# Three slots in place of two for the gathered rows of the second convolution

## What is computed

```
q = (x @ qw + qb); k = (x @ kw + kb); v = (x @ vw + vb)      # 8 heads of 16
alpha = sum(q[dst] * k[src]) / 4                             # per head
a = exp(alpha - max over dst);  a = a / (sum of a over dst)
out = segment_sum(v[src] * a, dst) + x @ sw + sb
x = layernorm(x + out)
```

## Time and profile before

| | |
|---|---|
| timed runs | 3534.03, 3537.03, 3537.83 us; median 3537.03 |
| profiled execution | span 3610.8 us, 73.8 us above the median; the page gives no other time for it |
| busy, share of the span | PE 75%, DVE 73%, ACT 56%, POOL 52% |
| the second convolution | from about 1271 to 1935 us |

### The profile page before, as it was taken

The page is one execution under the profiler, slowest core; times in us unless marked ns, Lnnn a source line. Parts: engine busy times, 40 slices in busy tenths (PEclk is TensorE's granted clock), DMA queues, the critical chain, the costliest instruction groups (busy, mean ns, idle before and its releaser), DMA issues. The chain is left out here.

```text
span 3610.8 us, 49441 instructions
## 1 busy us (share of the span) xinstructions
PE 2722.1 (75%) x14325; PEld 1795.7 (50%) x14325; DVE 2619.5 (73%) x3171; ACT 2007.5 (56%) x3400; POOL 1867.7 (52%) x1771
## 2 busy tenths in 40 slices
PE   7799999969999867777774789999999774233332
PEld 3466655646666645555553245566566553122211
DVE  6589888979999958888885159989989994222222
ACT  0166666645555547777784257788788783111111
POOL 4478776333333266666663655444553003667675
PEclk9999999989999979999997899999999996555565
DMA  6356656556666546666662156666666563222221
GB/s 201 95 183 213 198 188 197 185 174 196 199 196 198 171 151 204 201 199 199 202 207 85 49 133 185 178 192 181 185 192 182 171 181 104 56 60 73 64 69 41
DMA packets 474715, 572.34 MB, mean 159 GB/s; under 512 B 65347, under 2 KB 283133, under 8 KB 474431
## 3 DMA queue, kind: packets, MB, share of 16 engines
q1 hardware_dynamic: 412744, 457.19, 41.2%
q0 software_dynamic: 56480, 111.88, 11.6%
q10 hardware_dynamic: 5334, 1.32, 0.2%
HBM read 353.51 MB, written 220.55 MB: 159 GB/s over the span
## 5 line engine op out<-in xcount | busy, mean ns | idle before, releaser
L1302 POOL DMA_INDIRECT g_xd_xs<-table_x,dst_row x196 | 216.0, 1102 | 371.0 <-PE g_psT L1368 257.4
L1814 POOL DMA_INDIRECT f_xs<-table_x,src_row x196 | 191.2, 975 | 311.9 <-POOLq L1226 252.4
L785 POOL DMA_INDIRECT c_xs<-table_x,src_row x196 | 185.6, 947 | 303.9 <-PE c_psT L926 250.6
L775 POOL DMA_INDIRECT c_xs<-table_h,src_row x196 | 199.8, 1020 | 200.9 <-PE c_psT L919 103.7
L1877 ACT ACTIVATE f_reluT<-f_psY 128x512 f32<-128x512 f32 x49 | 29.3, 597 | 487.9 <-DMA table_x<-g_x3o 328.1
L507 POOL DMA_INDIRECT xs<-in_x,src_i x196 | 230.0, 1174 | 131.1 <-PE psT L588 61.9
L1821 POOL DMA_INDIRECT out<-f_xo,end_i x196 | 199.1, 1016 | 130.3 <-DVE f_xo L1914 70.1
L492 POOL DMA_INDIRECT xd<-in_x,dst_i x196 | 213.1, 1087 | 97.1 <-issue 48.5
L1302 POOL DMA_INDIRECT g_xd_xs<-table_x,src_row x196 | 219.1, 1118 | 59.8 <-issue 59.8
L775 POOL DMA_INDIRECT c_xd<-table_h,dst_row x196 | 212.1, 1082 | 59.8 <-issue 59.8
L1851 PE MATMUL f_psE<-w_center,f_reluT 128*128 128x128 f32 x392 | 84.7, 383 | 192.4 <-ACT f_reluT L1877 119.0
(11 more groups left out here) (330 smaller groups left out, 8603.2 us busy)
## 6 DMA issues: line engine op xcount, KB each, us to landing
g_share<-shares SPq DMA_DIRECT2D x196, 192.0 KB
xn<-in_x SPq DMA_DIRECT2D x49, 512.0 KB
table_x<-xo SPq DMA_DIRECT2D x49, 512.0 KB
table_x1b<-xb SPq DMA_DIRECT2D x49, 512.0 KB
c_xn<-table_x SPq DMA_DIRECT2D x49, 512.0 KB
table_h<-c_xo SPq DMA_DIRECT2D x49, 512.0 KB
c_xn<-table_h SPq DMA_DIRECT2D x49, 512.0 KB
c_x1r<-table_x1b SPq DMA_DIRECT2D x49, 512.0 KB
```

The costliest lines, as they stand in the source:

```text
L775: pool.indirect_dma_start(out=quarters(rows[:, s, :])[j], out_offset=None, in_=table, in_offset=edge_index(columns, now.n, j)).then_inc(la ...
L785: pool.indirect_dma_start(out=quarters(xs[:, s, :])[j], out_offset=None, in_=table, in_offset=edge_index(h.src_row, now.n, j)).then_inc(sr ...
L1302: pool.indirect_dma_start(out=quarters(xd_xs[:, s, k, :])[j], out_offset=None, in_=table, in_offset=edge_index(columns, now.n, j)).then_in ...
L1814: pool.indirect_dma_start(out=quarters(xs[:, s, :])[j], out_offset=None, in_=table, in_offset=edge_index(h.src_row, now.n, j)).then_inc(sr ...
```

## The change

The rings `xs` and `xd` of the second convolution get three slots (`PAIR_SLOTS`) in place of two. POOL's waits and PE's waits count by three, and POOL's wait for the turned rows is for tile n - 3. The turned copies `xsT` and `xdT` keep two slots. `d_landed` and `on_landed` get a third member too, which this layer doesn't use.

```diff
+PAIR_SLOTS = 3
 def gather_pair(nc, pool, h, now, table, xs, xd, src_landed, dst_landed, turned, per_step):
-    s = now.slot
-    wait(pool, src_landed[s], 64 * now.half)
-    wait(pool, dst_landed[s], 64 * now.half)
-    wait(pool, turned, per_step * (now.n - 2) + 2)
+    s = now.at(PAIR_SLOTS)
+    wait(pool, src_landed[s], 64 * now.turn(PAIR_SLOTS))
+    wait(pool, dst_landed[s], 64 * now.turn(PAIR_SLOTS))
+    wait(pool, turned, per_step * (now.n - PAIR_SLOTS) + 2)
...
-        d_slots, t_slots = (3, 6) if spread else (2, 2)
+        d_slots, t_slots = (3, 6) if spread else (PAIR_SLOTS, 2)
+        x_slots = 2 if spread else PAIR_SLOTS
-        xs, xd = sb("xs", [P, 2, TILE]), sb("xd", [P, d_slots, TILE])
+        xs, xd = sb("xs", [P, x_slots, TILE]), sb("xd", [P, d_slots, TILE])
...
+        src_landed, dst_landed = ([sem(f"{n}{s}") for s in range(x_slots)] for n in ("src_landed", "dst_landed"))
...
-                    turn(0, now, xs[:, s, :], src_landed[s], 64 * (now.half + 1))
-                    turn(1, now, xd[:, s, :], dst_landed[s], 64 * (now.half + 1))
+                    g, landed = now.at(x_slots), 64 * (now.turn(x_slots) + 1)
+                    turn(0, now, xs[:, g, :], src_landed[g], landed)
+                    turn(1, now, xd[:, g, :], dst_landed[g], landed)
```

More of the change, by code:

```diff
@@ L826, in conv @@
         psE = [bank(f"psE{k}") for k in range(3)]
-        far_landed, src_landed, dst_landed, node_landed, x1n_landed, x1e_landed, node_stored, edge_stored = [
+        src_landed, dst_landed = ([sem(f"{n}{s}") for s in range(x_slots)] for n in ("src_landed", "dst_landed"))
+        far_landed, node_landed, x1n_landed, x1e_landed, node_stored, edge_stored = [
             [sem(f"{n}{s}") for s in range(2)] for n in
-            ("far_landed", "src_landed", "dst_landed", "node_landed", "x1n_landed", "x1e_landed", "node_stored",
+            ("far_landed", "node_landed", "x1n_landed", "x1e_landed", "node_stored",
              "edge_stored")]
```

## The result

The changed kernel takes 3540.63 us (median of 20 runs, 3531.3 to 3551.23); the kernel before took 3534.18 us beside it (20 runs). The ratio is 1.0022, 95% interval 1.0013 to 1.0031: slower by 0.22%, which is 7.8 us (the medians are 6.5 us apart). The forecast was 3536 and "same", with 1.1 us gained; what came is a loss clear of the noise. It has the sign and about the size of the first rival, to which I had given 0.2. The measured time lies inside the range of 3530 to 3548 only because that range was stretched to take in this rival.

What follows compares the result with a forecast made beforehand. No engine was taken as full; a ring of waits between engines bounds the second convolution's step. Terms 0 + 0 - 1.1 + 0 = -1.1 us took the median 3537.0 to 3536, range 3530 to 3548.

Steps and rivals of the forecast that it cites:

- the first rival: Start of second convolution: POOL's first train, eight gathers longer, holds PE's results back; 10.0 us slower, 3547; chance 0.2.
- The steady part: Second convolution's regular steps: gathers start at the same moment behind a turn, same bytes; cost 0.
- The sign of being wrong: Second convolution's steady step, 13.06 us: a move by more than 0.15 us would show the prediction wrong.
- The fill: Start of second convolution: gathers from tile 3 on come earlier, train of 32, PE waited for none; cost 0.
- The drain: End of second convolution: POOL finishes one step earlier, so tile 47's turn is served sooner; -1.1 us.
- Slots, semaphores, addresses: Second convolution's extra semaphores, SBUF tiles and PE's wait count: no instruction added to a computing engine; cost 0.
- The faster rival: Second convolution: gathers set the pace, so POOL's pauses of 103.7 us are given back, 3433; chance 0.03.
- the mix in the fill: Some six tiles at the stage's start: loads and gathers meet otherwise, 6.8 us either way, 3530 to 3544; chance 0.07.

Runs made afterwards that it cites:

- the kernel paced as two: The changed kernel's three slots and addresses, but POOL still waits for the turn of tile n-2 as in the kernel before; 3537.54 us, ratio 0.9992.

## Why the prediction was wrong

- *The steady part, cost 0:* right, for the change. POOL starts a tile's gathers behind a turn as before, tile 27's at 1565.45 us behind the turn of tile 24, and the steps equal those of the kernel paced as two (12.86 us each). The sign of being wrong that I had set, a step that moves by more than 0.15 us, did appear (13.06 to 12.80), but it came from the two profiles' different conditions and not from the change.
- *The fill, cost 0:* this is the step that failed. I showed rightly that PE waits for none of the gathers that come earlier, and that tile 3's would follow without a pause to make a train of 32. What I did not charge is what the train does to others while it runs. It costs 10.3 us from the turn of tile 0 to that of tile 5 (81.8 against 71.5 us in the kernel paced as two) and 7.8 us in the timed ratio, which contains the drain's gain. The first rival had the mechanism in the main, and the size: 10.0 us. Its "22 us in place of 12.3" for DVE's first wait came in two, 8.49 and 14.72 us, as the first half of the products got through while the train still ran. My own timetable of the fill shows the slip: it has tile 1's turn copied at 1304.52, inside a train that lasts to 1311.2, though that copy had come 3.7 us behind a train's end. In the trace it came 4.7 us behind the end of the longer one, and tile 4's gathers waited for it.
- *Why I gave it 0.2:* for two reasons, and both were weak. The key that came through at 1289.21 showed only that not everything is kept back from the train's first moment; the same happens at 1243.40 here, in a kernel that then waits 26.81 us. And I took the 73.8 us by which the profiled execution was over the timed runs for something the profiler adds. The profile after has 3539.5 us of span and 3540.63 timed, and in every run here whose profiled execution was timed as well, that time is within 2 us of its span. In the last session the kernel before took 3609.88 us timed, near the 3610.8 of its profile. So the surplus is most likely the condition of the chip and not the profiler's doing, and the timed losses with 32 and 56 gathers show that the hold is in timed runs too. Besides, the drain's term rests on the same effect, a turn that meets a train's end and is served late; I counted it where it gave a gain and left it at nothing where it gave a loss.
- *The drain, -1.1 us:* right in the profile, 1.71 us to 0.64 (1.68 in the kernel paced as two). Too small to be seen in the time.
- *Slots, semaphores, addresses, cost 0:* right, 0.9992 [0.9981, 1.0002] with all of them and the short train.
- *The faster rival:* excluded. Where nothing is kept back, six slots take every pause from POOL for 360 gathers, and the ratio is 0.9999 and 1.0003; where results are kept back they cost 1.4%. On *the mix in the fill* no run shows a trace of it.

**What stays open.** That the loss grows with the train is shown (24, 32, 56 gathers), and so is the release by an opening. The change itself was timed in one session where results are kept back, 20 runs. What it is that is late is not shown: PE's signals are late by the record of semaphores, but the ends of matmuls are modelled, so the profile can't tell finished products from a PE that finishes late itself, or from a signal that travels late. An opening stops the making of gathers and lets the rows under way land, so no run separates these two. Nor is it known why results are kept back in one session and not in another. Sessions listed under one chip number have the kernel before at 3341.86, 3532.57, 3541.03 and 3609.88 us, so what I call a kind of chip may be a condition that comes and goes. The granted clock offers no explanation so far: over the first 1200 us, ahead of the stage, it is 0.98 of full speed both in the profile after and in that of the change where nothing is kept back; over the whole span it is 0.90 and 0.92.

## What to carry to other kernels

A buffer more for an engine that waits was worth nothing here, as nobody waited for that engine. It wasn't free either: it turned a pause into an unbroken burst, and a burst has to be charged with what it does to the others' hand-overs. When a trace has a long wait that ends with a burst, take the burst for its cause until something excludes it, and price any change that lengthens it. And compare a surplus of the profile over the timed runs with other runs of the same kernel before calling it the profiler's.

## What was not expected of the hardware

- The same kernel takes 3341 us on some chips or at some times, 3533 to 3541 and 3610 at others. A stage whose step is 11.38 us in the first has 12.7 to 13.1 in the others.
- In the first, unbroken trains of 144 and 360 indirect gathers delay nobody (DVE waits 1.00 us). In the others ACT's first long wait is 15.75 us with a train of 24, 26.81 with 32 and 50.53 with 56.
- Meanwhile the DMA engines are busy 18% of the time (1247 to 1265 us of the profile after), so it isn't a want of DMA bandwidth.
- Kept-back results come through singly and in PE's order, 6 to 21 us apart, during a train of 56; the first of them 0.8 us after the end of an opening of 2.1 us; only in part in openings of 0.7 and 1.2 us.
